# The end of a decoder layer on one core: late tiles in own buffers, X plus beta made earlier, the last rows sent ahead of a root

## The reference

```python
logits = einsum('bsd,ed->bse', tgt, Wr) + br            # 8 experts
top_v, top_i = top_k(logits, 2); top_w = softmax(top_v)
h = relu(einsum('bsd,efd->bsef', tgt, W1) + b1)         # 512 hidden
o = einsum('bsef,edf->bsed', h, W2) + b2
tgt2 = einsum('bsed,bse->bsd', o, router_w)
y = layer_norm(tgt + tgt2) * gamma + beta               # inner norm
x = layer_norm(tgt + y)                                 # outer norm
```

## Time and profile before

| | |
|---|---|
| median of 3 runs | 676.63 us (676.59 to 677.73) |
| the profiled execution | 676.38 us, span 674.6 us |
| busy share of the span | PE 79%, DVE 77%, POOL 72%, ACT 68% |
| units 0 to 38, first Relu to last result | 486.2 to 629.3 us |
| from there to the span's end | 45.3 us |

### The profile page before, as it was taken

One profiled execution on the slowest core, in us unless ns is written; L12 is line 12 of the kernel. 1 busy time (PEld: TensorE's weight loads), 2 busy tenths in 40 slices (PEclk: granted clock), 3 DMA queues, 4 the chain that ended last, 5 costly groups with the idle time before them and its releaser, 6 DMA issues.

```text
span 674.6 us, 19683 instructions
## 1 busy us (share of the span) xinstructions
PE 532.8 (79%) x6500; PEld 434.0 (64%) x6500; DVE 517.0 (77%) x1549; ACT 461.0 (68%) x987; POOL 485.8 (72%) x668
## 2 busy tenths in 40 slices
PE   1699999999997477888798888888789999997100
PEld 0388878887887355656576666665578888886100
DVE  3888898889875667688768989888759666677584
ACT  4988898989865465777757777765445555677325
POOL 5798878887877465575678989984576776577553
PEclk9799999999999766999969999986789999999555
DMA  6922222221223343535301010000322433721332
GB/s 168 252 23 25 25 24 25 23 23 22 25 40 106 149 168 131 226 143 215 110 20 39 24 36 28 20 24 24 100 90 61 116 109 89 211 60 52 96 100 63
DMA packets 113108, 55.43 MB, mean 82 GB/s; under 512 B 70624, under 2 KB 103840, under 8 KB 113024
## 3 DMA queue, kind: packets, MB, share of 16 engines
q1 hardware_dynamic: 103984, 25.46, 17.2%
q10 hardware_dynamic: 4496, 19.02, 7.2%
q0 software_dynamic: 4544, 9.84, 4.2%
HBM read 21.25 MB, written 33.05 MB: 80 GB/s over the span
## 4 chain that ended last, share of the span: by engine, by line
PE 35%; DVE 19%; ACT 14%; issue 14%; POOL 11%; DMA 4%; DVEq 1%; SPq 1%; ACTq 0%; POOLq 0%
PE PS L1033 7%; PE PS L1144 3%; POOL prod L797 3%; PE PS L1243 3%; ACT W_raw L1624 3%; ACT prod L1632 3%; PE PS L1155 3%; POOL ys L924 3%; PE PS L1335 2%; PE PS L1352 2%; PE PS L1354 2%; PE PS L1337 2%; ACT X L1553 2%; PE PS L1336 2%; PE PS L1353 1%
## 5 line engine op out<-in xcount | busy, mean ns | idle before, releaser
L1033 PE MATMUL PS<-prod,ident 128*128 128x144 f32 x1024 | 133.8, 289 | 7.1 <-DVE hctx L1939 6.8
L1033 PEld LDWEIGHTS PS<-prod,ident 128*128 128x128 f32 x1024 | 128.0, 191 | 14.9 <-issue 9.6
L797 POOL TENSOR_TENSOR prod<-prod,v 128x2048 f32<-128x2048 f32 x32 | 117.5, 3673 | 13.9 <-ACT prod L1449 13.9
L924 POOL DMA_INDIRECT ys<-W_raw,ids x78 | 76.6, 982 | 31.2 <-issue 18.0
L2209 DVE TENSOR_REDUCE m<-PS 128x8 f32<-128x1024 f32 x64 | 77.8, 1216 | 27.0 <-PE PS L1155 26.9
L1155 PE MATMUL PS<-prod 49*128 49x128 bf16 x1024 | 66.5, 234 | 26.5 <-issue 12.8
L2318 DVE SCALAR_TENSOR_TENSOR W_raw<-PS,W_raw 128x512 f16<-128x512 f32 x78 | 52.3, 689 | 37.2 <-ACT W_raw L1689 37.2
L864 POOL DMA_INDIRECT xs<-Y,spot_u x64 | 64.0, 1000 | 22.9 <-issue 14.8
L1962 DVE TENSOR_REDUCE PS<-pair_sq 128x128 f32<-128x1024 f32 (+1 forms) x44 | 74.8, 1700 | 1.9 <-ACT pair_sq L1514 1.9
L1624 ACT ACTIVATE W_raw<-PS 128x1024 f32<-128x1024 f32 x64 | 65.8, 1028 | 13.0 <-PE PS L1160 13.0
L1155 PEld LDWEIGHTS PS<-prod 49*128 49x128 bf16 x1024 | 42.2, 101 | 46.2 <-issue 18.9
(11 more groups left out here) (319 smaller groups left out, 1540.6 us busy)
## 6 DMA issues: line engine op xcount, KB each, us to landing
xs<-pad ACTq DMA_DIRECT2D x16, 1152.0 KB, 4.6
Y<-xs SPq DMA_DIRECT2D x39, 144.0 KB
W_raw<-ys SPq DMA_DIRECT2D x16, 256.0 KB, 3.9
W_raw<-in_L_ffn_W_dram SPq DMA_DIRECT2D x1, 2048.0 KB
shuffle<-hctx SPq DMA_DIRECT2D x32, 64.0 KB, 3.0
Y<-shuffle SPq DMA_DIRECT2D x32, 64.0 KB, 1.7
cs<-in_ctx_dram SPq DMA_DIRECT2D x8, 256.0 KB, 3.1
out_dram<-W_raw SPq DMA_DIRECT2D x8, 256.0 KB, 2.3
```

What stands on the lines that cost most here:

```text
L797: pool.tensor_tensor(rows[:, :, 0:D].rearrange("p t (d h) -> p t d h", d=HD), a.broadcast_to((P, H, HD, H)), v.broadcast_to((P, H, HD, H)) ...
L924: pool.indirect_dma_start(ys[:], bass.IndirectOffsetOnAxis(ap=ids[:, j % KD, s:s + 1].bitcast(U32), axis=0), ou[j % OD][:, s, :], None).th ...
L1033: last = pe.matmul(PS[:, 6, 0:TC], ident[:], prod2[:, i % 2, TC * t:TC * (t + 1)], start=(t == 0), stop=(t == H - 1))
```

## The change

Five edits, all in the experts' stage.

1. Tiles 4 to 7 get `zb` and `yb` of their own, in the space of `pair_sq`, which is free by then. `load_rows` no longer waits for a store, and SP issues the loads of tiles 4 to 7 in one go after the last send, before it stores tiles 2 and 3.
2. POOL's `center(3)` goes from behind the send of unit 36 to behind the last send. DVE's own `center(3)` goes behind the second statistics of tile 2, and its `finish(2)` ahead of `scale_rows(3)`.
3. A unit's list rows are loaded two to a partition: partition p takes rows 2p and 2p+1, 1152 contiguous bytes, where it took rows p and p+128.
4. X plus beta goes to a buffer of its own (`X_beta`, in the space of `prod2`), tile by tile, after the sends of units 6, 8, ... 20, and no longer stands in `center`.
5. DVE's `add_shifted` reads `X_beta`.

```diff
+        X_beta = prod2[:].rearrange("p a b -> p (a b)")[:, 0:T * NT].rearrange("p (t i d) -> p t i d", t=T, i=TB)
+        FIRST_BETA = 6
+        late = pair_sq[:].rearrange("p a b -> p (a b)")
-        zb = [rows2[:, NT * n:NT * (n + 1)].rearrange("p (i d) -> p i d", i=TB) for n in range(4)]
+        zb = [home[:, NT * n:NT * (n + 1)].rearrange("p (i d) -> p i d", i=TB) for home in (rows2, late) for n in range(4)]
...
-                sp.dma_start(xu[j % XD], xs[bass.ds(row, U), :].rearrange("(s p) r -> p s r", p=P)).then_inc(unit_in[j % XD], 16)
+                sp.dma_start(xu[j % XD], xs[bass.ds(row, U), :].rearrange("(p s) r -> p s r", s=2)).then_inc(unit_in[j % XD], 16)
...
-                if t >= 4:
-                    sp.wait_ge(stored[n], 16)
-                for a, buffer in enumerate((zb[n], yb[n])):
+                for a, buffer in enumerate((zb[t], yb[t])):
...
-            for t in range(4, 6):
+            for t in range(4, T):
                 load_rows(t)
-            for t in range(2, 4):
-                store_tile(t)
-                load_rows(t + 4)
-            for t in range(4, T):
+            for t in range(2, T):
                 store_tile(t)
...
             def add_beta(t):
 
-                pool.wait_ge(y_summed, t + 1)
-                pool.tensor_tensor(X[:, TB * t:TB * t + TB, :], X[:, TB * t:TB * t + TB, :],
+                if t == 0:
+                    after(pool, score_psum, 2 * B)
+                    after(pool, scoreT_psum, 2 * B)
+                after(pool, x2_ready, t + 1)
+                pool.tensor_tensor(X_beta[:, t], X[:, TB * t:TB * t + TB, :],
                                    bet[:].unsqueeze(1).broadcast_to((P, TB, D)), ALU.add).then_inc(x2_beta, 1)
 
             def center(t):
 
                 invert(t, ve3, rstd3, ve3_ready, rstd3_ready)
-                add_beta(t)
...
+                t, n = divmod(j - FIRST_BETA, 2)
+                if 0 <= t < T and n == 0:
+                    add_beta(t)
                 t, n = divmod(j - FIRST_FINAL + 1, FINAL_STEP)
-                if 0 <= t < EARLY and n == 0:
+                if 0 <= t < EARLY - 1 and n == 0:
                     center(t)
...
+            center(EARLY - 1)
             finish(EARLY - 2)
             finish(EARLY - 1)
...
-                step(dve.tensor_tensor(z, z, X[:, TB * t:TB * t + TB, :], ALU.add))
+                step(dve.tensor_tensor(z, z, X_beta[:, t], ALU.add))
...
-            center(EARLY - 1)
             fourth_stats(EARLY - 2)
             join_fourth(EARLY - 2)
+            center(EARLY - 1)
+            finish(EARLY - 2)
             scale_rows(EARLY - 1)
-            finish(EARLY - 2)
             finish(EARLY - 1)
```

More of the change, by code:

```diff
@@ L383, in decoder_layer @@
                        for n in part] for part in ((0, 1), (2, 3)))
+        X_beta = prod2[:].rearrange("p a b -> p (a b)")[:, 0:T * NT].rearrange("p (t i d) -> p t i d", t=T, i=TB)
+        FIRST_BETA = 6
         rows2 = W2_raw[:].rearrange("p a b -> p (a b)")
-        zb = [rows2[:, NT * n:NT * (n + 1)].rearrange("p (i d) -> p i d", i=TB) for n in range(4)]
-        yb = [rows2[:, NT * n:NT * (n + 1)].rearrange("p (i d) -> p i d", i=TB) for n in range(4, 8)]
+        late = pair_sq[:].rearrange("p a b -> p (a b)")
+        zb = [home[:, NT * n:NT * (n + 1)].rearrange("p (i d) -> p i d", i=TB) for home in (rows2, late) for n in range(4)]
+        yb = [home[:, NT * n:NT * (n + 1)].rearrange("p (i d) -> p i d", i=TB) for home in (rows2, late) for n in range(4, 8)]
         bn3 = sb("bn3", [P, 4, TB, 6])
@@ L620, in store_tile @@
                 sp.wait_ge(o4_ready, t + 1)
-                sp.dma_start(out[TB * t:TB * (t + 1)].rearrange("b s d -> s b d"), zb[t % 4]).then_inc(stored[t % 4], 16)
+                sp.dma_start(out[TB * t:TB * (t + 1)].rearrange("b s d -> s b d"), zb[t]).then_inc(stored[t % 4], 16)
             for t in range(FULL - 2, FULL):
@@ L1712, in normalise @@
                 for i in range(TB):
-                    last = act.activation(zb[t % 4][:, i, :], zb[t % 4][:, i, :], ACT.Identity, bias=shift3[:, t % 4, i:i + 1],
+                    last = act.activation(zb[t][:, i, :], zb[t][:, i, :], ACT.Identity, bias=shift3[:, t % 4, i:i + 1],
                                           scale=rstd3[:, t % 4, i:i + 1])
@@ L1720, in normalise_again @@
                 for i in range(TB):
-                    last = act.activation(zb[t % 4][:, i, :], zb[t % 4][:, i, :], ACT.Identity, bias=shift4[:, t % 4, i:i + 1],
+                    last = act.activation(zb[t][:, i, :], zb[t][:, i, :], ACT.Identity, bias=shift4[:, t % 4, i:i + 1],
                                           scale=rstd4[:, t % 4, i:i + 1])
@@ L2323, in add_second @@
             def add_second(t):
-                z = zb[t % 4]
+                z = zb[t]
                 dve.wait_ge(yrow_in[t % 4], 16 * 2 * (t // 4 + 1))
-                step(dve.tensor_tensor(z, z, yb[t % 4], ALU.add))
+                step(dve.tensor_tensor(z, z, yb[t], ALU.add))
             def add_input(t):
-                z = zb[t % 4]
+                z = zb[t]
                 settle()
@@ L2338, in third_stats @@
                 need(dve, n3_ready, t - 3)
-                row_stats(zb[t % 4], bn3[:, t % 4])
+                row_stats(zb[t], bn3[:, t % 4])
             def join_third(t):
@@ L2374, in fourth_stats @@
                 need(dve, o4_ready, t - 3)
-                row_stats(zb[t % 4], bn4[:, t % 4])
+                row_stats(zb[t], bn4[:, t % 4])
             def join_fourth(t):
```

## The result

The changed kernel takes 671.78 us, median of eight runs (670.04 to 674.39), against 676.50 for the kernel before in eight runs (674.47 to 678.17): ratio 0.9942, 95% interval 0.9920 to 0.9963. A second set of twelve runs, made later, gave 0.9944 (0.9909 to 0.9979). The sign was right, the size was not.

What follows compares the result with a forecast made beforehand. After the units, the last send's rows, then DVE's pace through the tail, were taken to bound the kernel. Tile 4 0.83 later and DVE's tail 2.26 shorter gave -1.43 us: 675.2 us, range 673.4 to 676.9.

Steps and rivals of the forecast that it cites:

- first root, POOL late (normalising of tile 0): First root: additions bring POOL 3.3 us late, 1.3 of it slack, so ACT's normalising of tile 0 comes 2.0 us later.
- blocked weight copies gone: Units 30 and 33: without additions, DVE's weight copies are not blocked; shifts of tiles 1 and 2 come sooner, 0.75 us off.
- last sends ahead of tile 3's root: Last units: sends go before tile 3's root, rows land 1.2 us sooner, but tile 4 starts at 640.7, 0.83 us later.
- own buffers: DVE's tail: waits of 0.13 and 1.37 us go, and 0.76 for a slowed instruction, 2.26 us off.
- the 5.7 us to spare: POOL's sends up to unit 27: at 2.54 us each it would send at 581.2, but sent at 586.86.
- the rival at 673.2: POOL catches up before unit 27, so the 2.0 us at the first root are gone: 673.2 us, chance 0.17.
- The second cost of late sends: Unit 28: SP loads tile 0's rows later, DVE stands 0.5 to 1.7 us, costed at nothing.
- The 0.76 counted for the slowed addition: DVE's tail, tile 6: an instruction takes 1.45 us beside POOL's beta addition, its like 0.69; moving the additions saves 0.76.
- The rival of dearer additions: POOL, units 6 to 20: additions take up to 1.62 us, POOL 2.9 us later at the first root: 678.1 us, chance 0.12.
- The stall moved from the rows to the root: Start of tile 4: it waits for tile 3's second root and shift instead of its rows, 640.7 against 639.87.
- Load form: Units' list-row loads: two rows per partition halve the pieces and leave the bytes; taken as 0.
- Tile 6 late: DVE's tail: eight loads in one go land late, the 1.37 us wait for tile 6 stays: 676.6 us, chance 0.16.

Runs made afterwards that it cites:

- e12: The changed kernel run once more, unchanged, for a second profile and ratio: ratio to before 0.9944, median 671.17 us.
- e3: The changed kernel with the load's form put back to rows p and p+128: ratio to before 0.9941, median 672.87 us.
- e11: The kernel before run once more, unchanged, for a second profile: 676.18 us in its one run.
- e1: The kernel before with only the new load form, two list rows to a partition: ratio to before 1.000, median 676.24 us.
- e2: The kernel before with only own buffers for tiles 4 to 7 and eight loads in one go: ratio to before 0.9957, median 672.91 us.
- e4: The changed kernel with the eight additions back behind POOL's first roots, still into their own buffer: ratio to before 0.9975, median 673.94 us.
- e5: The changed kernel with tile 3's root back behind the send of unit 36 and DVE's old order: ratio to before 0.9947, median 672.02 us.
- e9: Changed kernel, tiles 4 to 7's additions at the end, tile 3's first and tile 2's second root between sends of units 37 and 38: ratio to before 0.9910.

## Why the prediction was right in sign and wrong in size

The table gives every step in the prediction's own terms, now against the mean of the profiles whose code is the same in that column:

| step | forecast | profiles |
|---|---|---|
| first root, POOL late (normalising of tile 0) | +2.0 | +0.1 (write to N0: 70.3, mean of changed, e12, e3; 70.2, mean of before, e11, e1, e2, e4) |
| blocked weight copies gone | -0.75 | -0.9 (24.8 to 23.9) |
| last sends ahead of tile 3's root | -0.42 (0.83 less 2.0, plus 0.75) | -0.6 (22.5 to 21.9) |
| own buffers | -2.26 | -2.5 (29.6 to 27.1) |
| sum | -1.43 | -3.9 |

**The step that failed is the price of the backlog at the first root**: "the normalising goes from 592.63 to 594.6, 2.0 us later". The mechanism was there. POOL came to the root with no idle time, an addition cost 1.16 between two sends (from 526.49 to 528.92, 2.43 instead of 1.27; 1.22 was forecast), and the twice-made additions show that a longer list of POOL's moves the root. The distance was nearly right as well: 593.3 counted from the write at 524.01 is 69.3, and 68.7 was measured. What was wrong is what it was set against. I took the 5.7 us to spare, and DVE's readiness at 66.0, from one execution in which PE did not wait for list rows. In e11, the same kernel, and in e1, e2 and e4, which have no additions ahead of the root either, PE does wait, and DVE is ready at 66.8 to 69.0. The root comes at the later of two times, POOL's 68.7 to 69.2 or DVE's 66 to 69; a delay of POOL costs only what it stands out over the other. The prediction added it to the earliest of five.

Counting from unit 27's result, which is where PE stands, shows it most plainly. ACT's result of unit 27 and normalising of tile 0, in e11, then in e12, then in e3:

```profile
585.15 0.62 ACT L1705 ACTIVATE W_raw<-PS,w_rows 128x128 f32<-128x128 f32 x2 [0.60 <-PE PS L1354]
...
592.30 1.65 ACT L1713 ACTIVATE W_raw<-W_raw,shift,rstd 128x128 f32<-128x128 f32 x4 [0.20 <-DVE shift L2355]
```

```profile
584.87 0.63 ACT L1709 ACTIVATE W_raw<-PS,w_rows 128x128 f32<-128x128 f32 x2 [0.62 <-issue]
...
593.42 1.65 ACT L1717 ACTIVATE W_raw<-W_raw,shift,rstd 128x128 f32<-128x128 f32 x4 [1.54 <-issue]
```

```profile
587.63 0.62 ACT L1709 ACTIVATE W_raw<-PS,w_rows 128x128 f32<-128x128 f32 x2 [0.62 <-issue]
...
594.58 1.64 ACT L1717 ACTIVATE W_raw<-W_raw,shift,rstd 128x128 f32<-128x128 f32 x4
```

Without additions ahead of the root the normalising comes 7.14 to 7.16 behind unit 27's result, in all five profiles (before, e1, e2, e4, e11), wherever PE stands. With all eight it comes 8.15 (changed) and 8.55 (e12) behind where PE is early, 61.9 and 61.5 after the last list write, and 6.95 (e3) where PE is late, 64.0. So the backlog cost 1.0 and 1.4 in two executions and nothing in the third, not 2.0. The kernel before and e12 have PE at the same place, 61.5: there the cost was 1.4, and the 0.6 that is missing from the forecast's 2.0 is POOL's list, shorter than forecast.

The mean of these three is +0.7, not the +0.1 of the table; the other 0.6 is that PE happened to stand later in the five profiles (63.1 on average) than in these three (62.5), and no row ties that to an edit. With +0.7 the sum is -3.3, with +0.1 it is -3.9, and the interval of the time, 2.5 to 5.4 us less, holds both. Either way the price of 2.0 is the main part of the miss, and the rest is that the other three steps each gave 0.15 to 0.25 more than forecast. That the first profile was the earliest of five was chance, as far as these runs show; taking it for the kernel's own was the error. The outcome is close to the rival at 673.2 ("the backlog costs nothing"), though not by its reason: POOL's sends came hardly closer than before (2.52 a unit, 573.97 to 576.49, against 2.54).

The second cost of late sends, the rows of tile 0, was put at nothing and came out so: DVE waited 0.85 for them in the changed kernel (584.05) and 0.80 in e12 (585.55), within the forecast's 0.5 to 1.7 us, and the root still found POOL with no idle time.

The single pair of profiles would have misled the other way: 4.7 us less, of which 2.2 lie ahead of unit 27's result, where both kernels do the same. Part of that is seen in the clock (before, PE waited 2.49 at 498.80 and its clock fell to 0.78 to 0.79 in 498 to 506; after, 1.17 at 497.51 and no fall), and two more profiles have the order reversed, 520.7 for the kernel before (e11) and 523.4 for the changed one (e12), and there it is the changed kernel whose clock fell (0.63 and 0.81 in 499 to 505). No row ties it to an edit.

**Own buffers**: right, and 0.2 more; part of that is that an instruction that waits for nothing starts before its predecessor has ended (640.45 against 640.37 + 0.17). The 0.76 counted for the slowed addition went, but not because the additions had moved (e2).

**Weight copies**: 0.9 for the two copies ahead of tiles 1 and 2, not 0.75. Among the units only one of the eight additions met a copy in the changed kernel's profile. The views of line 2307 (count, ns min/median/max), of that copy, and of line 936 of the changed kernel:

```profile
L2307 DVE SCALAR_TENSOR_TENSOR w_rows<-Y x26: 147/152/1402, 527.4 to 614.9; 128x2 f32<-128x2 f32 x26
```

```profile
527.39 1.40 DVE L2307 SCALAR_TENSOR_TENSOR w_rows<-Y 128x2 f32<-128x2 f32 x1
```

```profile
L936 POOL TENSOR_TENSOR prod<-X,bet x8: 1272/1280/1287, 527.5 to 571.2; 128x512 f32<-128x512 f32 x8
```

One of 26 copies took 1.40 us beside an addition of 1.28 (527.48) and ended 0.03 behind it. The Trainium skill (SBUF — State Buffer, Who interferes with whom) calls this an exclusive lock on a port pair, and the row agrees. The rival of dearer additions falls: 1.27 to 1.29 each.

**Last sends ahead of the root**: the chain was right to 0.05 us. Unit 38's result at 627.44, a send 0.76 later (628.20), the root at 630.44, DVE's scaling of tile 3 3.0 long, the second root at 636.48, tile 4 at 637.60; the forecast's steps give 637.62 from the same result. "The stall moved from the rows to the root" holds. What I did not see is that, once the additions were gone, the old place of the root did as well: in e5's profile this stretch is shorter, and the whole is the same.

**Load form**: nothing, as forecast. **Tile 6 late**: did not happen; SP issues the eight loads within 5.43 us:

```profile
631.76 5.43 SPq L616 DMA_DIRECT2D pair_sq<-ys  x8
```

**The range** failed with the same step: it allowed the backlog to cost nothing with every other step as forecast, but held no term for the difference between two executions of the kernel before, which was visible in no single profile.

What stays open: why PE's wait near 498 us, the last list write and PE's place at unit 27 differ between executions of one kernel, and how often PE is early. The clock falls at different places in each, and no run here controls it.

## What to carry to other kernels

Work that is moved onto an engine ahead of a meeting point costs only what it stands out beyond the other engine's arrival; read that arrival from several executions before it is taken as fixed, and count from the last event that ties both engines together, not from the start of the span. When a wait is traced to "the instruction ahead of it in the queue", ask which of those instructions: here it was mostly the additions that held the sends, and moving the root as well gained nothing that shows. Gaps in a queue near its end (2.6 us on POOL before the last two sends) are places to try for short steps of the next tile: e9 shortened its stretch by about 2 us that way.

## What was not expected of the hardware

After a wait of PE near 525 to 531 us (1.15 to 2.56 us long) the granted clock fell in six of the ten profiles that have such a wait, and not by its length alone: a wait of 2.55 us (e1) was followed by 0.72 in 529 to 535, one of 2.56 (e3) by 1.00 throughout. Windows (us, busy, granted clock, DMA share, GB/s) of e3, which hold the second part of its wait, then of e1, just behind its wait:

```profile
529.00:532.00 3.00, 1.15 (x16) 1.00 0.51 141
532.00:535.00 3.00, 3.00 (x43) 1.00 0.63 168
```

```profile
529.00:532.00 3.00, 3.00 (x33) 0.72 0.62 175
532.00:535.00 3.00, 3.00 (x31) 0.72 0.58 180
```

And an addition on POOL beside DVE's tail cost DVE 0.76 us in the kernel before and nothing in others with the same additions (e2, e4), where no DVE addition or scaling of the tail is longer than 0.70 and POOL's roots are the ones that take longer (1.38 to 1.53 us against 1.0): which instruction pays depends on which two meet.
